# A graph network on one core: the tensor engine no longer stops for its own every seventh select to mark a choice buffer as used

## The chip, the cores and the metric

One core of a Trainium2 chip runs one program. The time is device time in microseconds (us) of one execution. The engines are PE (TensorE matmul; PEld is its weight load), DVE (VectorE), ACT (ScalarE), POOL (GpSimd) and SP (SyncE, which here only issues transfers). They run side by side and are ordered by semaphores alone.

## The reference

A graph of 6250 nodes with 128 features and 200,000 edges goes through two blocks, each on top of a layer norm and a residual add:

```python
edge_index = jnp.stack([src, dst])
h = jnp.maximum(_layernorm(x), 0.0)
# block L0: a learned mask for every edge, and a weighted mean of the neighbours
hid = relu(h[src] @ W1[:d] + h[dst] @ W1[d:] + b1)
mask = sigmoid(hid @ W2 + b2)
agg = segment_sum(mask * h[dst], src) / segment_sum(mask, src)
x = x + relu((0.5 * h + 0.5 * agg) @ Wl + bl)
# block L1: four layers; the greatest neighbour, by feature
h = jnp.maximum(_layernorm(x), 0.0)
for layer in range(4):
    agg = segment_max(h[src], dst)
    h = relu(agg @ W + b + h @ R)
x = x + h
```

## The kernel before

Nodes are sorted by their number of edges into 49 tiles of 128, and the tiles into 7 ranges of 7 (896 nodes). A neighbour's row reaches its node in two ways.

The first is a **select** on PE. For each range (7) and each source tile (49) a one-hot matrix of 128 x 896 fp8 values, the choice, picks at most one row of the source tile for each node of the range. The source rows are split into three bf16 parts, so that a select is six matmuls: three parts by two column groups (512 and 384). One pass over all nodes is 7 x 49 = 343 selects. The second way is a **gather** on POOL: an indirect DMA that fetches one row for each of 128 nodes. One pass has 430 of them, into a ring of rows in SBUF.

Two phases use this pattern. Phase A (in the trace from about 819 us to 2229 us) makes the edge masks of block L0: 343 selects. Phase C (from about 3267 us to the end) is the four layers of block L1: 4 x 343 = 1372 selects and 1720 gathers. Between them lies phase B, which the change does not touch.

In phase C the engines do the following, each in an order that was written out by hand.

- PE runs `select(layer, n)` (L2151 to L2170) for n = 0..342. It waits for the choice block when n is a multiple of seven, and for `taken`, so that it is at most three selects ahead of DVE (three PSUM buffers `wide`). Then come six matmuls on L2164; the last counts `selected`. Between selects PE also has the transposes and products of a range (`turn_own` L2147, `turn_staged` L2185, `multiply` L2196 and L2197, `turn_back` L2208).
- DVE runs `take(layer, n)` (L2249, L2252): it waits for `selected` and takes the maximum of `wide` into `even` or `odd`. Between takes it reduces gathered tiles (L2276, L2281) and counts `reduced`.
- POOL runs `gather_tile` (L2032 to L2040; the gather is L2038). Before a tile it waits for the reduction that frees its place in the ring. After a range it stores the new rows (L2049).
- SP runs `load_choice(n)` (L1972 to L1977): a choice block holds seven selects (`CHUNK = 7`), there are three buffers, and the fourth and later loads wait until a buffer is used. Loads of source tiles and own rows stand behind these waits in SP's order.
- ACT converts source tiles and applies bias and relu.

A choice buffer counts as used in this way: after every seventh select PE waits until its own select has been counted and then counts `choice_used`:

```python
last.then_inc(selected, 1)
if s % CHUNK == CHUNK - 1:
    pe.wait_ge(selected, no + 1)
    pe.sem_inc(choice_used, 1)
```

Phase A has the same lines (L1329 to L1331). There the choice is made by DVE (`compare`, L1395 to L1402) three selects ahead of its take, and it is `compare` that waits for `choice_used` at the first select of a block, from the fourth block on. PE has two PSUM buffers in phase A and also the products of `dot`; DVE's take is L1411.

Of the kernel before, what the change touches and what calls it, by code (L numbers as in the profile page):

```python
# [122 lines left out]
def gnn(nc, x_in, src_in, dst_in, w1_in, b1_in, w2_in, b2_in, wl_in, bl_in,  # L123
# [20 lines left out]
    with ExitStack() as whole:  # L144
# [11 lines left out]
        sb, ps, sem = tensors(whole)  # L156
# [51 lines left out]
        with nc.cleanup_on_exit(), ExitStack() as ctx:  # L208
            sb, ps, _ = tensors(ctx)
            sem = nc.alloc_semaphore  # L210
# [168 lines left out]
        with nc.cleanup_on_exit(), ExitStack() as ctx:  # L379
            sb, ps, _ = tensors(ctx)  # L380
            sem = nc.alloc_semaphore
# [295 lines left out]
        with ExitStack() as ctx:  # L677
            sb, ps, sem = tensors(ctx)
# [104 lines left out]
        with ExitStack() as ctx:  # L783
            sb, ps, sem = tensors(ctx)
# [132 lines left out]
        with ExitStack() as ctx:  # L917
            sb, ps, sem = tensors(ctx)
# [105 lines left out]
        CHUNK = RANGE  # L1024
# [48 lines left out]
        with nc.cleanup_on_exit(), ExitStack() as ctx:  # L1073
            sb, ps, _ = tensors(ctx)
            sem = nc.alloc_semaphore
# [37 lines left out]
            parts_made = sem("a_parts_made")  # L1113
            pick_loaded = [sem(f"a_pick_loaded{e}") for e in range(A_PICKS)]
            choice_made = sem("a_choice_made")
            choice_used = sem("a_choice_used")
            choice_stored = [sem(f"a_choice_stored{e}") for e in range(3)]
            selected = sem("a_selected")
            taken = sem("a_taken")
# [186 lines left out]
            @block.tensor  # L1306
            def _(pe):
                def turn_own(a, h, first, count):
                    pe.wait_ge(own_loaded[a], 16)
                    if a or h:  # L1310
                        pe.wait_ge(bt_made, 2 * a + h)
                    for c in range(count):
                        last = pe.transpose(turned[:, c, :], own_b[:, a * RANGE + first + c, :], ident[:, :])
                    last.then_inc(own_turned, 1)

                def select(n):
                    a, s, q, e = n // TILES, n % TILES, n % 2, n // CHUNK % 3
                    if a == 0 and s % CHUNK == 0:
                        pe.wait_ge(parts_made, 3 * (s // CHUNK + 1))
                    pe.wait_ge(choice_made, n + 1)  # L1320
                    if n >= 2:
                        pe.wait_ge(taken, n - 1)
                    for part in range(3):
                        for lo_c, hi_c in ((0, BANK), (BANK, RCOLS)):
                            last = pe.matmul(wide[q][:, lo_c:hi_c], parts[:, s, part, :],  # L1325
                                             choice[e][:, s % CHUNK, lo_c:hi_c], start=(part == 0),
                                             stop=(part == 2))
                    last.then_inc(selected, 1)
                    if s % CHUNK == CHUNK - 1:  # L1329
                        pe.wait_ge(selected, n + 1)  # L1330
                        pe.sem_inc(choice_used, 1)  # L1331

                def dot_own(a):
                    pe.wait_ge(bt_made, 2 * a + 2)
                    if a:
                        pe.wait_ge(masks_made, a)
                    for lo_c, hi_c in ((0, BANK), (BANK, RCOLS)):
                        pe.matmul(logits[:, lo_c:hi_c], minus_w2[:, :],
                                  minus_bt[:, a * RCOLS + lo_c:a * RCOLS + hi_c], start=True, stop=False)

                def dot(a, first, count):

                    pe.wait_ge(taken, a * TILES + first + count)
                    for lo_c, hi_c in ((0, BANK), (BANK, RCOLS)):
                        for s in range(first, first + count):
                            g, row = s % COLS, s // COLS
                            last = pe.matmul(logits[g * WIDTH:(g + 1) * WIDTH, lo_c:hi_c],  # L1347
                                             w2_col[:, WIDTH - 1 - row:2 * WIDTH - 1 - row],
                                             hidden[(a * TILES + s) % A_HIDDEN][:, lo_c:hi_c], start=False,
                                             stop=(s >= TILES - COLS), tile_position=(0, g * WIDTH))  # L1350
                            if lo_c:
                                last.then_inc(dotted, 1)

                def turn_masks(a, h, first, count):
                    pe.wait_ge(masks_made, a + 1)
                    if a or h:
                        pe.wait_ge(masks_copied, 2 * a + h)
                    for c in range(count):
                        last = pe.transpose(mask_turned[:, c, :], mask_t[:, (first + c) * P:(first + c + 1) * P],
                                            ident[:, :])  # L1360
                    last.then_inc(masks_turned, 1)

                for half in HALVES:
                    turn_own(0, *half)
                pe.wait_ge(w_loaded, (3 + 3) * 16)
                pe.wait_ge(w2_clear, 2)
                for n in range(SELECTS):
                    a, s = n // TILES, n % TILES
                    select(n)
                    if s == 0:  # L1370
                        if a:
                            dot(a - 1, FOURS, TILES - FOURS)
                        dot_own(a)
                    elif s % COLS == 0:
                        dot(a, s - COLS, COLS)
                    if a < RANGES - 1 and s in TURN_AT:
                        turn_own(a + 1, *HALVES[TURN_AT.index(s)])
                    for half, at in zip(HALVES, MASK_AT):
                        if a and s == at[1]:
                            turn_masks(a - 1, *half)  # L1380
                dot(RANGES - 1, FOURS, TILES - FOURS)
                for half in HALVES:
                    turn_masks(RANGES - 1, *half)

            @block.vector
            def _(dve):
# [8 lines left out]
                def compare(n):  # L1395
                    m, s = n // CHUNK, n % CHUNK
                    dve.wait_ge(pick_loaded[n % A_PICKS], (n // A_PICKS + 1) * 16)
                    if s == 0 and m >= 3:
                        dve.wait_ge(choice_used, m - 2)
                        dve.wait_ge(choice_stored[m % 3], m // 3 * 16)  # L1400
                    dve.tensor_scalar(choice[m % 3][:, s, :], pick_row[n % A_PICKS][:, :], one_up[:, :], None,  # L1401
                                      ALU.is_equal, saturate=False).then_inc(choice_made, 1)  # L1402
# [79 lines left out]
                for n in range(3):  # L1482
                    compare(n)
# [4 lines left out]
                for n in range(SELECTS):  # L1488
                    a, s = n // TILES, n % TILES
# [73 lines left out]
        with ExitStack() as ctx:  # L1563
            sb, ps, sem = tensors(ctx)
# [327 lines left out]
        with ExitStack() as ctx:  # L1892
            sb, ps, sem = tensors(ctx)
# [29 lines left out]
            far_used = sem("c_far_used")  # L1923
            far_did = sem("c_far_did")
            choice_loaded = [sem(f"c_choice_loaded{e}") for e in range(3)]
            choice_used = sem("c_choice_used")
            source_loaded = [sem(f"c_source_loaded{e}") for e in range(2)]
            rest_made = sem("c_rest_made")
            parts_made = sem("c_parts_made")
            selected = sem("c_selected")  # L1930
# [34 lines left out]
            def _(sp):  # L1965
# [6 lines left out]
                def load_choice(n):  # L1972
                    a, c, e = n // CHUNKS_OF % RANGES, n % CHUNKS_OF, n % 3
                    if n >= 3:
                        sp.wait_ge(choice_used, n - 2)
                    sp.dma_start(choice[e][:, :, :].bitcast(U8),
                                 chosen[a, :, c * CHUNK:(c + 1) * CHUNK, :]).then_inc(choice_loaded[e], 16)  # L1977

# [160 lines left out]
            def _(pe):  # L2139
# [11 lines left out]
                def select(layer, n):  # L2151
                    a, s = n // TILES, n % TILES
                    no, m = layer * SELECTS + n, (layer * SELECTS + n) // CHUNK
                    q, e = no % 3, m % 3
                    if a == 0 and s % CHUNK == 0:
                        pe.wait_ge(parts_made, 3 * (layer * CHUNKS_OF + s // CHUNK + 1))
                    if s % CHUNK == 0:
                        pe.wait_ge(choice_loaded[e], (m // 3 + 1) * 16)

                    if no >= 3:  # L2160
                        pe.wait_ge(taken, no - 2)
                    for part in range(3):
                        for lo_c, hi_c in ((0, BANK), (BANK, RCOLS)):
                            last = pe.matmul(wide[q][:, lo_c:hi_c], parts[:, s, part, :],  # L2164
                                             choice[e][:, s % CHUNK, lo_c:hi_c], start=(part == 0),
                                             stop=(part == 2))
                    last.then_inc(selected, 1)
                    if s % CHUNK == CHUNK - 1:
                        pe.wait_ge(selected, no + 1)
                        pe.sem_inc(choice_used, 1)  # L2170

                def turn_staged(layer, a, h, first, count):
                    no = range_no(layer, a)
# [226 lines left out]
```

## Time and profile before

| | us |
|---|---|
| median of 3 runs | 6895.0 |
| lowest, highest | 6875.02, 6910.07 |
| span of the profiled execution | 6939.9 |

The profiled execution's own time is known by its span, from its first to its last instruction; it lies 44.9 us above the median of the runs.

Busy time by engine in the profiled execution: PE 3939.7 us (57%), DVE 4021.9 us (58%), POOL 3259.7 us (47%), ACT 858.7 us (12%). No engine is busy throughout, so the busy shares alone name no bound; the waits between the engines have to be read. In the timelines consecutive instructions of a kind are merged into one row; matmuls overlap each other, and their ends are modelled. In brackets stands the idle time of the engine before the row and who ended it; "remote" is a release that the profile can't put down to an instruction, "issue" is no wait that it shows.

### The profile page before, as it was taken

How to read it: one execution, taken by the hardware profiler on the slowest of the kernel's cores; microseconds unless marked ns; L12 is line 12 of the kernel's file. 1: busy time of each engine (PE TensorE's matmuls, PEld its weight loads, DVE VectorE, ACT ScalarE, POOL GpSimd, SP SyncE). 2: the span in 40 equal slices, each digit the busy share in tenths (PEclk: the TensorE clock that was granted, in tenths of full speed). 3: DMA queues.
4: the chain of work that ended last, by engine and by line, in shares of the span. 5: the costliest groups of instructions: out<-in, count | busy, mean ns of one | idle time of the engine just before them, and what ended most of it. 6: DMA issues, size and time to landing. Idle time of an engine off the chain costs nothing.

```text
span 6939.9 us, 51665 instructions
## 1 busy us (share of the span) xinstructions
PE 3939.7 (57%) x16577; PEld 1823.3 (26%) x16577; DVE 4021.9 (58%) x6785; ACT 858.7 (12%) x2421; POOL 3259.7 (47%) x3300
## 2 busy tenths in 40 slices
PE   7631255535544698995565554565655565555565
PEld 5411122112211244442222221222222222222232
DVE  7799266535654688885555454454555454454454
ACT  0000000000000567763000001000010000000000
POOL 0300456756766334334455445555446555444544
PEclk9999577767777899997787777777777777687787
DMA  6468444323432899996322223222233222322221
GB/s 252 170 251 327 126 117 120 108 75 106 120 96 77 168 182 200 194 185 137 89 87 87 78 78 90 77 85 78 80 85 86 80 84 78 86 82 79 80 87 59
DMA packets 367939, 820.12 MB, mean 118 GB/s; under 512 B 101885, under 2 KB 222547, under 8 KB 367491
## 3 DMA queue, kind: packets, MB, share of 16 engines
q0 software_dynamic: 145712, 329.41, 21.7%
q1 hardware_dynamic: 172564, 408.70, 17.1%
q10 hardware_dynamic: 49392, 78.70, 3.9%
q8 instruction: 133, 2.18, 0.1%
q14 instruction: 138, 1.13, 0.0%
HBM read 579.98 MB, written 236.57 MB: 118 GB/s over the span
## 4 chain that ended last, share of the span: by engine, by line
PE 20%; another core or an unknown queue 20%; issue 7%; DVE 5%; POOL 0%; DMA 0%; ACT 0%; DVEq 0%; POOLq 0%
PE c_wide L2164 18%; DVE c_even L2252 2%; DVE c_ring L2276 1%; DVE c_odd L2252 1%; PE c_product L2196 1%; PE c_product L2197 1%; DVE c_source L2239 0%; PE c_turned L2208 0%; PE c_turned L2185 0%; DVE c_best_t L2259 0%; POOL table L2049 0%; DVE c_even L2249 0%; DVE c_staged L2281 0%; DMA c_source<-table 0%
## 5 line engine op out<-in xcount | busy, mean ns | idle before, releaser
L2164 PE MATMUL c_wide<-c_choice,c_parts 128*128 128x512 fp8e4 (+1 forms) x8232 | 1909.8, 392 | 1617.2 <-remote 727.9
L2038 POOL DMA_INDIRECT c_ring<-table,near x1720 | 1657.7, 964 | 995.4 <-issue 521.4
L2164 PEld LDWEIGHTS c_wide<-c_choice,c_parts 128*128 128x128 bf16 x8232 | 835.3, 106 | 2666.0 <-issue 1565.2
L2252 DVE TENSOR_TENSOR c_even<-c_even,c_wide 128x896 f32<-128x896 f32 x672 | 728.3, 1084 | 834.9 <-remote 635.6
L2252 DVE TENSOR_TENSOR c_odd<-c_odd,c_wide 128x896 f32<-128x896 f32 x644 | 698.0, 1084 | 778.1 <-remote 568.3
L1325 PE MATMUL a_wide<-a_choice,a_parts 128*128 128x512 fp8e4 (+1 forms) x2058 | 512.9, 398 | 506.2 <-DVE a_hidden L1411 265.5
L1411 DVE TENSOR_TENSOR a_hidden<-a_wide,a_minus_bt 128x896 f32<-128x896 f32 x343 | 372.0, 1085 | 623.3 <-remote 492.0
L1204 POOL DMA_INDIRECT a_ring<-table_a,near x430 | 470.1, 1093 | 450.1 <-DVE a_value L1472 279.3
L1733 PE MATMUL b_agg<-b_mass,b_h_row 128*128 128x512 f32 (+1 forms) x1372 | 595.3, 571 | 140.7 <-DMA b_mass<-masks 140.1
L1694 ACT ACTIVATE b_mass<-b_onehot,mask_r 128x128 f32<-128x128 bf16 x2058 | 625.5, 387 | 265.0 <-DVE b_onehot L1756 264.9
L1672 POOL DMA_DIRECT2D b_mass<-masks x343 | 297.4, 867 | 548.0 <-ACT b_mass L1694 508.4
L1211 POOL DMA_INDIRECT masks<-a_value,a_cell x430 | 447.2, 1040 | 138.7 <-issue 130.4
L1325 PEld LDWEIGHTS a_wide<-a_choice,a_parts 128*128 128x128 bf16 x2058 | 201.8, 106 | 827.0 <-issue 686.3
L2103 ACT ACTIVATE c_h_t<-c_product,c_b 128x512 f32<-128x512 f32 (+1 forms) x56 | 35.5, 634 | 2848.4 <-PE c_product L2197 2518.2
L1733 PEld LDWEIGHTS b_agg<-b_mass,b_h_row 128*128 128x128 f32 x1372 | 260.1, 198 | 455.5 <-issue 251.4
L2049 POOL DMA_INDIRECT table<-c_new,row_info x147 | 144.2, 981 | 501.2 <-ACT c_new L2112 466.1
L1778 DVE TENSOR_TENSOR b_pile<-b_pile,b_mass 128x896 f32<-128x896 f32 x224 | 244.3, 1091 | 159.4 <-DMA b_mass<-masks 158.7
L1756 DVE TENSOR_TENSOR b_onehot<-pick_of,up_row 128x768 bf16<-128x768 bf16 x343 | 326.2, 951 | 0.1
L1347 PE MATMUL a_logits<-a_hidden,a_w_col 128*32 128x512 f32 (+1 forms) x1372 | 189.4, 649 | 114.6 <-DVE a_hidden L1411 64.3
L2276 DVE TENSOR_TENSOR c_ring<-c_ring 128x256 f32<-128x256 f32 (+8 forms) x468 | 248.4, 531 | 0.3
L1401 DVE TENSOR_SCALAR a_choice<-a_pick_row,one_up 128x896 fp8e4<-128x896 bf16 x343 | 237.4, 693 | 0.0
L707 POOL DMA_INDIRECT meta<-record,rank x49 | 47.2, 963 | 381.8 <-DVE rank L777 367.4
(284 smaller groups left out, 3294.5 us busy)
## 6 DMA issues: line engine op xcount, KB each, us to landing
masks<-n_zeros SPq DMA_DIRECT2D x196, 784.0 KB, 20.5
b_mass<-masks POOLq DMA_DIRECT2D x343, 448.0 KB
c_choice<-chosen SPq DMA_DIRECT2D x196, 784.0 KB
a_pick_row<-picks ACTq DMA_DIRECT2D x343, 224.0 KB
chosen<-a_choice SPq DMA_DIRECT2D x49, 784.0 KB
c_ring<-table,near POOLq DMA_INDIRECT x1720
c_source<-table SPq DMA_DIRECT2D x28, 448.0 KB
a_ring<-table_a,near POOLq DMA_INDIRECT x430
```

The costliest lines, as they stand in the source:

```text
L1204: pool.indirect_dma_start(ring[:, at + j, :], None, table_a, bass.IndirectOffsetOnAxis(near[:, u, j:j + 1], 0)).then_inc(landed[u % A_FLOW ...
L1211: pool.indirect_dma_start(mask_cells, bass.IndirectOffsetOnAxis(cell[:, j:j + 1], 0), value[:, j:j + 1], None).then_inc(cells_stored, 16)
L1325: last = pe.matmul(wide[q][:, lo_c:hi_c], parts[:, s, part, :], choice[e][:, s % CHUNK, lo_c:hi_c], start=(part == 0), stop=(part == 2))
L1411: dve.tensor_tensor(hidden[n % A_HIDDEN][:, :], wide[n % 2][:, 0:RCOLS], minus_bt[:, a * RCOLS:(a + 1) * RCOLS], ALU.max).then_inc(taken, 1)
L1672: pool.dma_start(flat[e], masks[u * P:(u + 1) * P, cb * RCOLS:(cb + 1) * RCOLS], accum_op=ALU.add).then_inc(mass_loaded[e], 16)
L1694: last = act.mul(mass[k % M_RING][:, c, :], onehot[e][:, c, :], mask_r[:, u, cb * RANGE + c:cb * RANGE + c + 1])
L1733: last = pe.matmul(agg[cb % 2][:, lo_c:hi_c], h_row[:, u, :], flat[e][:, lo_c:hi_c], start=(u == 0), stop=(u == TILES - 1))
L1756: dve.tensor_tensor(onehot[e][:, :, :], bc(pick_of[:, u, first:first + SCALED].unsqueeze(2), full), bc(up_row[:, :].unsqueeze(1), full), A ...
L2038: pool.indirect_dma_start(ring[:, at + j, :], None, table1[layer % 2], bass.IndirectOffsetOnAxis(near[:, u, j:j + 1], 0)).then_inc(landed[ ...
L2164: last = pe.matmul(wide[q][:, lo_c:hi_c], parts[:, s, part, :], choice[e][:, s % CHUNK, lo_c:hi_c], start=(part == 0), stop=(part == 2))
L2252: dve.tensor_tensor(side[:, :], side[:, :], found, ALU.max).then_inc(taken, 1)
L2276: halves.did(dve.tensor_tensor(lower, lower, upper, ALU.max))
```

## The change

PE's wait for its own seventh select and its count of `choice_used` go away in both phases, and so does the semaphore. Who refills a buffer, DVE's `compare` in phase A and SP's `load_choice` in phase C, waits for the count of selects itself: for seven times the number of blocks that must be done.

```diff
@@ phase A, PE select
                     last.then_inc(selected, 1)
-                    if s % CHUNK == CHUNK - 1:
-                        pe.wait_ge(selected, n + 1)
-                        pe.sem_inc(choice_used, 1)
@@ phase A, DVE compare
                     if s == 0 and m >= 3:
-                        dve.wait_ge(choice_used, m - 2)
+                        dve.wait_ge(selected, CHUNK * (m - 2))
                         dve.wait_ge(choice_stored[m % 3], m // 3 * 16)
@@ phase C, SP load_choice
                     if n >= 3:
-                        sp.wait_ge(choice_used, n - 2)
+                        sp.wait_ge(selected, CHUNK * (n - 2))
@@ phase C, PE select
                     last.then_inc(selected, 1)
-                    if s % CHUNK == CHUNK - 1:
-                        pe.wait_ge(selected, no + 1)
-                        pe.sem_inc(choice_used, 1)
```

There are 49 such places in phase A and 196 in phase C.

## Rows read from the trace of the kernel before

**Rows 1.** The page, parts 1 and 2: busy time, and granted clock by slice.
```profile
PE 3939.7 (57%) x16577; PEld 1823.3 (26%) x16577; DVE 4021.9 (58%) x6785; ACT 858.7 (12%) x2421; POOL 3259.7 (47%) x3300
PEclk9999577767777899997787777777777777687787
```

**Rows 2.** Busy time by engine in the first and last layer (granted clock, DMA share, GB/s).
```profile
3270.70:4168.00 897.30, 508.36 (x2249) 234.32 (x2247) 456.52 (x559) 37.69 (x58) 445.89 (x463) 0.76 0.29 83
...
5990.00:6940.00 950.00, 511.17 (x2212) 231.15 (x2212) 467.89 (x576) 27.99 (x35) 468.54 (x486) 0.75 0.28 80
```

**Rows 3.** Line views of L2164 and L2038, and PE's seventh wait, L2170 (ns minimum/median/maximum).
```profile
L2164 PE MATMUL c_wide<-c_choice,c_parts x8232: 323/379/634, 3266.9 to 6906.9; 128*128 128x512 fp8e4 x196
...
L2038 POOL DMA_INDIRECT c_ring<-table,near x1720: 941/947/1824, 3248.6 to 6888.2; - x192
...
L2170 PEldq EVENT_SEMAPHORE  x196: 51/51/51, 3303.1 to 6907.2; - x196
```

**Rows 4.** L2164: idle before it, by releaser (us, times); then who waited for it.
```profile
  remote: 727.9, 53
  DVE c_even L2252: 485.9, 179
...
  PE c_wide L2164: 35.8, 89
...
  PE c_turned L2208: 2.1, 7
  PE c_product L2196: 1.4, 4
```

**Rows 5.** Timeline of PE (start us, us, what), outside POOL's gathers.
```profile
3983.38 3.57 PE L2164 MATMUL c_wide<-c_choice,c_parts 128*128 128x512 fp8e4 x18 [0.30 <-PE c_wide L2164]
...
3988.51 4.70 PE L2164 MATMUL c_wide<-c_choice,c_parts 128*128 128x512 fp8e4 x24
3993.52 0.52 PE L2208 MATMUL c_turned<-ident,c_h_t 128*128 128x128 f32 x3 [0.30 <-PE c_wide L2164]
```

**Rows 6.** Timeline of DVE in the same stretch.
```profile
3984.12 0.95 DVE L2276 TENSOR_TENSOR c_ring<-c_ring 128x768 f32<-128x768 f32 x1
3984.99 1.08 DVE L2252 TENSOR_TENSOR c_even<-c_even,c_wide 128x896 f32<-128x896 f32 x1
...
3993.25 1.09 DVE L2252 TENSOR_TENSOR c_even<-c_even,c_wide 128x896 f32<-128x896 f32 x1
3995.21 1.09 DVE L2252 TENSOR_TENSOR c_odd<-c_odd,c_wide 128x896 f32<-128x896 f32 x1 [0.87 <-PE c_wide L2164]
```

**Rows 7.** DVE's takes (L2252 alone) in and behind one run of gathers, by window.
```profile
3866.00:3875.00 9.00, 6.91 (x7) 1.00 0.43 133
3875.00:3916.00 41.00, 3.96 (x4) 0.59 0.25 69
3916.00:3927.60 11.60, 6.35 (x6) 0.70 0.25 75
```

**Rows 8.** Timeline of PE in that run of gathers.
```profile
3874.06 2.43 PE L2164 MATMUL c_wide<-c_choice,c_parts 128*128 128x512 fp8e4 x12
3886.95 4.64 PE L2164 MATMUL c_wide<-c_choice,c_parts 128*128 128x512 fp8e4 x12 [10.46 <-remote]
...
3917.27 6.40 PE L2164 MATMUL c_wide<-c_choice,c_parts 128*128 128x512 fp8e4 x18 [12.98 <-DVE c_odd L2252]
```

**Rows 9.** Waits of SP's queue and of POOL: us in total, times, longest us.
```profile
SPq L1976 <- PEq L2170: 2839.6, 155, 50.9
...
POOL c_ring L2038 <- DVE c_staged L2281: 469.4, 37, 31.2
POOL table L2049 <- ACT c_new L2112: 466.1, 32, 30.2
```

**Rows 10.** L1325, phase A's select: idle before it, by releaser (us, times).
```profile
  remote: 134.0, 8
...
  PE a_wide L1325: 4.6, 11
```

More of the change, by code:

```diff
@@ L1115, in gnn @@
             choice_made = sem("a_choice_made")
-            choice_used = sem("a_choice_used")
             choice_stored = [sem(f"a_choice_stored{e}") for e in range(3)]
@@ L1925, in gnn @@
             choice_loaded = [sem(f"c_choice_loaded{e}") for e in range(3)]
-            choice_used = sem("c_choice_used")
             source_loaded = [sem(f"c_source_loaded{e}") for e in range(2)]
```

## The prediction, made before the changed kernel was run

> **What bounds the kernel now.** I read the busy shares first: PE and DVE are at 57% and 58%, so neither is full, and PE's granted clock is at seven tenths in most slices of phase C [rows 1]. A layer takes about 910 us with PE busy for 510, DVE for 460 and POOL for 450 to 470 of them [rows 2]. Three engines at half load that wait for each other make a chain, so I went on to the waits of the selects.
>
> PE's idle time before a select has two large parts: DVE's takes (485.9 us for the even ones), and 727.9 us in only 53 stops that the profile gives to nobody [rows 4]. The timeline shows what these 53 are. POOL issues gathers in runs; in the one that begins at 3866 us DVE gets through seven takes in the first 9.0 us, four in the next 41.0 us, while the gathers are in flight, and six (with two copies of a new range beside them) in the 11.6 us behind the run [rows 7]. Nothing else in DVE's order holds it there: each of the four takes starts as soon as its select is counted. PE issued two selects at 3874.06 and the next only 10.46 us after their modelled end [rows 8]. So a select that costs 1.13 us alone takes 7 to 15 us while many gathers are in flight, and PE falls idle enough that the granted clock drops to 0.59 in that window [rows 7]. Over the 78 runs of gathers in phase C it looks the same: about 10 to 14 takes to a run, whether it has 20 gathers or 50.
>
> The chain of phase C is then: in a run of gathers the time is POOL's (1720 gathers at 0.947 us and 0.30 us between them, 2145 us [rows 3]), and PE and DVE nearly stand. Between runs the time is PE's and DVE's: POOL waits for a reduction or for new rows, 469.4 and 466.1 us [rows 9], and the runs can't start before DVE has worked off its order. A microsecond of PE is worth a microsecond between the runs and in their first 9 us, if DVE isn't the later one, and almost nothing inside.
>
> **What the change removes.** At a seventh select PE stops until its own count is back. Rows 5 give the price. Twenty-four matmuls take 4.70 us and eighteen 3.57, so a select is 4.70 - 3.57 = 1.13 us, and the modelled end of a batch lies 3.57 - 3 x 1.13 = 0.18 us behind the place where the next select would begin. With the stop it begins 0.30 us after that end. One stop costs 0.30 + 0.18 = 0.48 us of PE. The wait's own instruction (51 ns [rows 3]) lies within it. If each of the 245 stops in both phases were paid in full, the gain would be 245 x 0.48 = 118 us; that is the upper end, and zero is the lower.
>
> How many are on the path:
> - In phase C 89 + 7 + 4 = 100 stops are ones in which PE's own select was what came last [rows 4], 48 us gross. DVE hides some. After the stop before 3983.38 DVE has a reduction of 0.95 us and takes the next select without a gap: hidden. After the one before 3993.52 DVE waits 0.87 us for PE: paid [rows 5, 6]. To count them all I laid phase C out select by select from the same records: a select starts at the latest of the select before it plus 1.13, the third take back, and (at a seventh) its own completion; a take starts at the later of its select and DVE's order; all that these terms don't explain stays as recorded. Without the own-completion term 75 of the 100 stops shorten the end, by 33.5 us together.
> - In 43 of the other 96 the profile names another releaser or none, but the same gap of 0.30 us mostly stands there. They give 12 us by the same reckoning.
> - The last 53 fall into stalls of gathers [rows 4]. Taken at face value they give 26 us. But inside a run the wall time is POOL's: work that PE begins 0.48 us earlier crawls 0.48 us longer. At the speed of rows 7 (four takes in 41 us, against one in 1.13) a tenth of it is left, some 3 us. Both ends, 3 and 26, go into the range; I take 3, since in rows 7 the takes stand still until the gathers have landed.
> - Phase A has 11 stops of this kind, 4.6 us of idle time [rows 10]. It has two PSUM buffers, so DVE's take is nearly always the later one; the reckoning gives 2 us, and 6 more at stalls, of which I take none.
>
> Sum: 33.5 + 12 + 3 + 2 = 50 us of 6939.9.
>
> **What it adds.** SP waits for `selected` in place of `choice_used`. It is still the seventh select that releases it, now by its own count and not by PE's instruction behind it, so a load is issued up to 0.1 us earlier. Behind that wait stand the loads of own rows and source tiles; none comes later. SP waits for the seventh select 155 times already [rows 9], and the buffer that it fills is needed two blocks, at least 14 x 1.13 = 16 us, later. Nothing is late next there: no row puts a PE stop down to a choice load. In phase A `compare` waits for select 7(m-2) when DVE has already taken select 7m-4: the wait is always met, and an equal wait stood there before. I cost both at nothing. If the cover went away, the price would be that of a late load, the length of a transfer.
>
> What is late next, once PE doesn't stop, is DVE: a take is 1.08 us at 1.0 us spacing when queued, plus reductions, against 1.13 us for a select. The two are so close that DVE is already behind at a quarter of the stops.
>
> **A rule weighed against the row.** The row says 0.48 us for a stop [rows 5]. The Trainium skill, "TensorE: Matmul & The Clock Gate", section "Single matmul latency", gives an isolated matmul (398 + N)/2.4 ns at the high clock, so the part that a stream hides is 398/2.4 = 166 ns; its section "Part 2: What happens when you issue a matmul" says that the drain of one matmul overlaps the fill of the next. If only that came back, 143 stops would be worth 0.166 us each, 24 us gross and 18 net by an estimate from this page, and the time would be about 6877. The 0.18 us of overlap in rows 5 agrees with it; the 0.30 us are on top of it, and the rule doesn't speak of them.
>
> **The rivals.**
> - *The stops inside the stalls count too.* If a stalled select has a fixed length from the moment it is issued, then issuing earlier brings all of it forward. For it: the 53 stops stand in front of long stalls. Against: the stalls end with the runs. Gain 33.5 + 12 + 26 + 8 = 80 us, time 6815.
> - *DVE or another wait takes the stop's place.* The layout keeps every other wait as recorded; if DVE's lag after a stop spreads more than it says, half or less of 50 is left, 10 to 30 us, time 6865 to 6885. For it: at 25 of the 100 stops it is so now, and the select behind a seventh also waits for a choice block and `taken`.
> - *Only the overlap comes back.* The next instruction has counted waits too (`taken`, a choice block); if reading them costs PE the 0.30 us of [rows 5] in any case, only 0.18 us of a stop are saved: 143 x 0.18 = 26 us, of which three quarters are on the path, 19 us, time 6876. Against it: selects within a block wait for `taken` and follow each other without a gap [rows 5]. The rule above gives nearly the same, 6877.
> - *Slower: the runs of gathers grow together.* Each run has 9 us in which PE and DVE go on at full speed, seven takes, before the stall sets in [rows 7]. Seven takes outside cost 7 x 11.6/8 = 10 us. POOL waits 69 times [rows 9]; if DVE frees the ring a little earlier, POOL may not come to rest and two runs become one, which loses one such start. From five lost starts on the 50 us are gone, and from nine on (90 - 50 = 40 us) the kernel is slower by over 0.5%, 6935. Against: the waits are 469.4/37 = 12.7 and 466.1/32 = 14.6 us long on average, and 0.48 us in seven selects closes only the shortest.
> - *It does nothing.* PE's next instruction waits for something that comes at the same moment: 6895.
>
> **How the numbers follow.** The profiled span is 6939.9, the median 6895.0; 50 us off the span are 0.72%, and 0.72% off 6895 give 6845. A measurement of this kernel can tell about 0.5% from no change, 34.5 us, so that "faster" begins at 6860.5. Chances: forecast (6830 to 6860, with a few runs just above) 0.46; stalls count too 0.18; DVE or another wait in its place 0.20; only the overlap comes back 0.05; runs grow together 0.07; nothing 0.04. Faster is the first two without the forecast's upper edge, 0.46 + 0.18 - 0.02 = 0.62; slower 0.07; the rest, 0.31, is the same. The range runs from 6800 (80 us and the 15 us by which the median can be off) to 6890 (10 us of gain, less 5 of scatter); it leaves out the slower case, no change at all and a little below.
>
> **What would show it.** In the profile after: no instruction on L2170's place; PE's "idle ended by its own select" near zero; rows like 3993.52 without the 0.30; DVE's idle time put down to L2164 down by some tens of us; the four layers shorter by about 12 us each, phase A by 2. The time in the 53 stalls should not change. A layer that is shorter by 20 us would say that the stalls count; fewer runs of gathers with longer ones among them would say that they grew together; unchanged layers with DVE idle less and PE idle more on `taken`, that DVE took the stop's place. The forecast is wrong if the stalls aren't tied to the gathers but to PE's own queue, since then the change reaches them.

## The result, and the profile after

The changed kernel takes 6807.1 us (median of 4 runs, 6786.0 to 6819.5), the kernel before beside it 6885.2 us. The ratio is 0.9874 with a 95% interval of 0.983 to 0.9917: 1.3% faster. In a later series it was 6807.6 against 6908.0 us, 0.9889 (0.9848 to 0.993). The forecast had the sign, and the time lies in its range, but the gain is 78 to 100 us where 50 were forecast.

First the page of the profile after, parts 1 and 2. Its span is 6809.3 us, 1.7 us below that execution's own time.

```profile
span 6809.3 us, 51420 instructions
...
PE 3987.8 (59%) x16577; PEld 1827.2 (27%) x16577; DVE 4012.4 (59%) x6785; ACT 858.9 (13%) x2421; POOL 3264.0 (48%) x3300
...
PEclk9999578776777798998777777777767776777777
```

The instruction counts are those of [rows 1], and the busy times lie within 50 us of them; it is idle time that is gone. The two spans differ by 131 us, more than the medians do, because the profiled execution of before was a long one.

The view of PE's select line in phase C: who ended its idle time (us, times).

```profile
L2159 PE MATMUL c_wide<-c_choice,c_parts x8232: 323/379/634, 3249.9 to 6776.6; 128*128 128x512 fp8e4 x196
...
  issue: 1819.0, 1702
  DVE c_odd L2244: 872.4, 250
  DVE c_even L2244: 665.6, 244
```

The rows of [rows 4] in which PE waited for itself (89 + 7 + 4 times) are gone, and so are the 53 that the profile gave to nobody. The idle time of these 53, 727.9 us, is not gone with them: most of it now stands under DVE's takes (1538.0 us against 873.2 before), so the stalls of PE in the runs of gathers are still there. What moved is their place. By the records PE sat idle for 1617 us before selects in the kernel before, 897 of it ahead of the first select of a block; after, it is 1466 us, and 284 of it there. The timeline of PE over a seventh select shows the change best.

```profile
3950.67 4.70 PE L2159 MATMUL c_wide<-c_choice,c_parts 128*128 128x512 fp8e4 x24
3955.21 0.49 PE L2200 MATMUL c_turned<-ident,c_h_t 128*128 128x128 f32 x3
3955.54 4.70 PE L2159 MATMUL c_wide<-c_choice,c_parts 128*128 128x512 fp8e4 x24
```

In [rows 5] the same three transposes stand 0.30 us behind the modelled end of the select before; here they begin 4.54 us after a batch that lasts 4.70, 0.16 us ahead of its end. From one batch's start to the transposes it was 5.01 us and is now 4.54, so the stop was worth 0.47 us, as predicted.

The waits of POOL and of SP's queue (us in total, times, longest us):

```profile
POOL table L2044 <- ACT c_new L2107: 443.3, 24, 31.3
POOL c_ring L2033 <- DVE c_staged L2273: 382.2, 35, 29.4
...
SPq L1971 <- PE c_wide L2159: 2039.0, 136, 46.1
```

POOL rests 110 us less between its gathers than in [rows 9] (443.3 + 382.2 against 466.1 + 469.4). SP waits for the select directly, as the last line shows.

Last the view that corresponds to [rows 7]: DVE's takes in and behind a run of gathers of the same length at the same place of the first layer, first the 9 us from its start, then 41 us, then 9 us.

```profile
3826.70:3835.70 9.00, 7.54 (x7) 1.00 0.43 135
3835.70:3876.70 41.00, 5.47 (x6) 0.64 0.25 69
3876.70:3885.70 9.00, 4.33 (x4) 0.76 0.46 140
```

In the 41 us there are six takes and not four. The run of [rows 7] begins with seven indirect stores of new rows (L2049, from 3865.98 us); its first gather is issued at 3874.99 us. So where this document speaks of a run of gathers, the stores that lead into it belong to it, and the 9 us count from the first of them.

The following table is reckoned from the instruction records of each trace: the time from a layer's first to its last take, added over the four layers, and the takes that fall between 9 us after a run of gathers has begun and 3 us after it has ended. A run is a row of indirect transfers of POOL, stores too, with no gap over 0.6 us. The pace outside is the rest of phase C's time, with the three changes of layer of 32 us each in it, divided by the rest of the takes; without these changes all its figures are about 0.08 us lower and their differences stay.

| trace | stops in C | four layers, us | takes in runs | us a take outside |
|---|---|---|---|---|
| before | 196, with count | 3542 | 336 | 1.601 |
| after | none | 3427 | 390 | 1.551 |
| e1_c_only | none | 3408 | 401 | 1.549 |
| e2_a_only | 196, with count | 3514 | 351 | 1.583 |
| e3_one_back | none, held one select back | 3410 | 403 | 1.547 |
| e4_stop_twice | 392, no count | 3494 | 380 | 1.618 |
| e5_stop_only | 196, no count | 3480 | 379 | 1.570 |
| e6_count_only | count, no stop | 3447 | 380 | 1.531 |
| e7_stop_third | 196, no count | 3429 | 405 | 1.574 |
| e8_stop_every | 1372, no count | 3589 | 338 | 1.758 |
| f1_after_again | none | 3408 | 398 | 1.533 |
| f2_stop_count | 196, with count | 3517 | 354 | 1.576 |
| f3_two_wide | none, two buffers | 3545 | 382 | 1.689 |

Traces of one program differ by some 20 us in the four layers (3408 to 3427 for the changed kernel, which was profiled twice). Phase A scatters more: 1345 to 1438 us over these traces, whether it has stops or not. The takes in runs hang on the definition in two rows: with gaps up to 1.0 us still counted as one run, e8_stop_every has 404 and f3_two_wide 390, while the others move by one at most.

### The profile page after: what moved, and what is told of

Its sections match the earlier page's. It is cut to its first block, busy times and chain, and to the rows that moved or that the text cites. A ratio compares the mean times of both kernels' runs of the same rounds, so it can differ in the third digit from the quotient of the medians.

```text
span 6809.3 us, 51420 instructions
## 1 busy us (share of the span) xinstructions
PE 3987.8 (59%) x16577; PEld 1827.2 (27%) x16577; DVE 4012.4 (59%) x6785; ACT 858.9 (13%) x2421; POOL 3264.0 (48%) x3300
## 3 DMA queue, kind: packets, MB, share of 16 engines
q0 software_dynamic: 145712, 329.41, 22.1%
q14 instruction: 138, 1.13, 0.0%
## 4 chain that ended last, share of the span: by engine, by line
PE 21%; another core or an unknown queue 19%; issue 7%; DVE 5%; DMA 0%; POOL 0%; ACT 0%; SPq 0%; DVEq 0%; POOLq 0%; ACTq 0%
PE c_wide L2159 19%; DVE c_even L2244 2%; DVE c_odd L2244 1%; DVE c_ring L2268 1%; PE c_product L2188 1%; PE c_product L2189 1%; DVE c_source L2231 0%; PE c_turned L2200 0%; PE c_turned L2177 0%; DMA c_source<-table 0%; POOL table L2044 0%; DVE c_best_t L2251 0%; DVE c_staged L2273 0%; ACT c_parts L2084 0%
## 5 line engine op out<-in xcount | busy, mean ns | idle before, releaser
L2159 PE MATMUL c_wide<-c_choice,c_parts 128*128 128x512 fp8e4 (+1 forms) x8232 | 1949.9, 397 | 1467.2 <-issue 636.8
L2044 POOL DMA_INDIRECT table<-c_new,row_info x147 | 147.1, 1000 | 480.8 <-ACT c_new L2107 443.3
```

## The experiments

Each series ran on one chip beside the kernel before. The record numbers the chips 2 (e1 to e4), 3 (e5 to e8), 3 again (e9 to e12), 8 (f1 to f4) and 10 (f5, f6). Where a diff says phase C, phase A is that of the changed kernel.

### Where the gain comes from

**e1_c_only and e2_a_only.** The changed text of phase C with the old phase A, and the reverse.

> The change in phase C alone; phase A keeps its 49 stops. Theory S (a stop costs PE 0.48 us wherever it stands, and inside a run of gathers it also costs progress of the stalled select, seen in the trace of after as 390 takes within runs against 336): nearly all of the 78 us come from phase C, so 6815 to 6825 us. Rival P (the prediction's own working: stops inside the runs are free, 48 us from phase C): 6837 us, and the rest of the 78 us would have to come from phase A.

> The change in phase A alone; phase C keeps its 196 stops. Theory S: phase A is 18 us shorter in the pair of traces, so 6865 to 6880 us. Rival P: 2 us, so 6883 us, the same as before.

Phase C alone: 6798.1 us against 6902.1, ratio 0.9844 (0.9801 to 0.9887). Phase A alone: 6900.9 us, ratio 0.9987 (0.9958 to 1.0016). All of the gain is in phase C. The 18 us that the first pair of traces showed in phase A were scatter; the forecast's 2 us can't be told from nothing. P's figure for phase C, 48 us, is too low by half against 104 us here. Theory S missed both times too: it took the 78 us for phase C and counted on 18 us from phase A.

### What a stop costs

**e3_one_back.** PE is held at a seventh select, but for the select before it.

```diff
                     last.then_inc(selected, 1)
+                    if s % CHUNK == CHUNK - 1:
+                        pe.wait_ge(selected, no)
```

> The changed kernel, and in phase C PE waits at every seventh select for the select before the one it has just issued, so that it is held but never runs empty. Theory S in the form 'an empty PE is what costs': one select is always in flight, so the time is that of the changed kernel, 6807 us, and the takes within runs stay near 390. Rival D (what counts in a run is how many selects PE has issued ahead): the hold takes one of two or three issued selects away, so part of the loss comes back, 6825 to 6850 us, with the interval before the take behind a seventh select above 5.4 us.

6803.0 us, the same as without any hold, with 403 takes in runs. The hold costs nothing as long as one select is in flight. So it is not the waiting instruction that costs; e7 below shows that not every stop that lets PE run empty costs something either.

**e5_stop_only, e6_count_only, e9_stop_count, f2_stop_count.** The two halves of the removed lines apart, and both together with SP left on its new wait.

```diff
 e5_stop_only
+                    if s % CHUNK == CHUNK - 1:
+                        pe.wait_ge(selected, no + 1)
 e6_count_only
+                    if s % CHUNK == CHUNK - 1:
+                        pe.sem_inc(choice_used, 1)
 e9_stop_count, f2_stop_count
+                    if s % CHUNK == CHUNK - 1:
+                        pe.wait_ge(selected, no + 1)
+                        pe.sem_inc(choice_used, 1)
```

> The changed kernel with one stop in seven in phase C (behind the seventh select) but without the count: SP still waits for the selects. Phase C alone was worth about 100 us, and 392 stops cost 87 us. Theory F (the first stop in seven costs all, the second is hidden or pays little): the loss is back, 6890 to 6905 us. Rival C (the stop costs 87/392 = 0.22 us each, and the rest of the 100 us was the count and who waits for it): 6807 + 196 x 0.22 = 6850 us.

> The changed kernel in which PE counts an extra semaphore at every seventh select of phase C, without waiting and with nobody waiting for the count. Theory F: one more short instruction on PE's sequencer, nothing, 6800 to 6815 us. Rival C: if the count is what cost, some of the 100 us come back, 6840 us or more.

> The changed kernel with PE's stop and count back in phase C and SP waiting for the selects. Where the kernel before takes about 6895 us: 6890 to 6905 us if PE's restart of 0.47 us is all there is, 6825 to 6845 us if SP's wait for the count made part of the loss. Where it takes about 5559 us: the same as before.

The stop alone: 6834.3 us against 6896.5, ratio 0.9905 (0.9873 to 0.9937), so about 27 us of the loss are back if e6 and e7, at 6805.2 and 6804.1 us, stand for the changed kernel in this series. The intervals of the ratios of e5 and e6 (0.9833 to 0.9894) overlap, so these 27 us are hardly clear of the scatter; e5 lies below what either theory expected. The count alone: 6805.2 us, nothing. Both: 6906.7 us against 6908.0, ratio 0.9997 (0.9968 to 1.0026), and everything is back. So PE's side is the whole of it, and SP's wait has no measurable part. By the records a stop alone lets PE's next matmul start 0.387 us after the start of its last one, against 0.163 without a stop: 0.22 us lost. With the count behind the wait it is 0.629 us: 0.47 us lost. Without a wait the count leaves it at 0.163 us (e6); why it costs 0.24 us more behind one was not tested. In phase C 196 stops of 0.22 us are 43 us gross, and 27 were paid; 196 of 0.47 us are 92 us gross, and 99 were paid (f2 against f1).

**e4_stop_twice, e7_stop_third, e8_stop_every.** Stops without a count behind the third and the seventh select, behind the third alone, and behind all.

```diff
 e4_stop_twice
+                    if s % CHUNK in (2, CHUNK - 1):
+                        pe.wait_ge(selected, no + 1)
 e7_stop_third
+                    if s % CHUNK == 2:
+                        pe.wait_ge(selected, no + 1)
 e8_stop_every
+                    pe.wait_ge(selected, no + 1)
```

> The changed kernel, with two stops in seven selects in phase C (behind the third and the seventh), twice as many as the kernel before had there. Theory S: about 68 us for 196 stops, so 392 stops give 6807 + 2 x 68 = 6943 us. Rival P: 48 us for 196 stops, so 6807 + 96 = 6903 us. If stops cost less when there are more of them (DVE's lag hides the second), below 6900 us.

> The changed kernel with one stop in seven behind the third select in place of the seventh, in phase C. If a stop costs the same wherever it stands, this equals the one behind the seventh. Theory F in the form 'a stop behind the seventh costs more, since the select behind it also waits for a choice block': 6820 to 6850 us here against 6890 to 6905 there. Theory S (0.48 us plus the lost progress in runs): the same in both places, 6870 to 6900 us.

> The changed kernel with a stop behind every select of phase C, 1372 of them. At 0.48 us of PE each, a select costs PE 1.13 + 0.48 = 1.61 us, above DVE's 1.08 us plus reductions, so nearly every stop between the runs is paid: about 1000 takes x 0.48 = 480 us less DVE's part, 7100 to 7300 us. If PE's look-ahead is what carries a select through a run of gathers, more: above 7300 us. If the cost saturates as from 196 to 392 stops, below 7000 us.

6894.2, 6804.1 and 6982.7 us. All three lie below what was expected of them by the price of 0.48 us. The timeline of PE in e8_stop_every shows four selects with a stop each in 5.41 us where they take 4.70 without, 0.71 / 3 = 0.24 us a stop (0.386 - 0.163 = 0.22 us by the records of all of them):

```profile
4025.15 5.41 PE L2159 MATMUL c_wide<-c_choice,c_parts 128*128 128x512 fp8e4 x24
```

I had counted 0.48 us for these stops too; without the count they are half as dear. 1372 stops of 0.22 us are 302 us gross, and 176 are paid. One stop in seven behind the third cost nothing that can be seen, behind the seventh about 27 us, and both about 90 (e4 against e1 and e3): by the medians more than the two apart. Theory F fails in its first form, since a second stop in seven costs more than the first. What fits is that a small bubble goes into the slack between PE and DVE and a larger one doesn't, but that was only argued; nor is it settled that the third place differs from the seventh, as the intervals of e5 (0.9873 to 0.9937) and e7 (0.9856 to 0.9922) overlap.

### Whether the gathers are what slows the selects

**e9_stop_count, e10_nogather_stop, e11_nogather_free, e12_two_wide.** In this series the kernel before itself took 5558.9 us; everything in it has to be read against that number. In e10 (the kernel before) and e11 (the changed kernel) POOL issues no gathers in phase C. DVE sets the ring to zero once and reduces what lies there, so the gathered neighbours are missing from the output:

```diff
                     if after > 0:
                         pool.wait_ge(reduced, after)
-                    for j in range(CAP[u]):
-                        pool.indirect_dma_start(ring[:, at + j, :], None, table1[layer % 2],
-                                                bass.IndirectOffsetOnAxis(near[:, u, j:j + 1], 0)
-                                                ).then_inc(landed[n % FLOWS], 16)
...
-                        dve.wait_ge(landed[n % FLOWS], LANDED[n])
```

> The changed kernel with PE's stop and its count back at every seventh select of phase C, while SP still waits for the selects: PE as before, SP as after. In the traces a stop alone makes PE restart 0.387 us after the start of its last matmul, against 0.163 without one (0.22 us lost), and a stop with the count behind it 0.629 us (0.47 us lost). Theory P2 (PE's restart is all there is): the whole loss is back, 6890 to 6905 us. Rival W (SP's wait for the count made part of the loss): as the stop alone, 6825 to 6845 us.

> The kernel before without the 1720 gathers of phase C: the ring is set to zero once, the reductions run on it, and the output lacks the neighbours that come by gathers. If gathers slow the selects, phase C falls from 3540 us to PE's and DVE's own time; DVE has 1855 us of work in 3669, so about 2100 to 2300 us for phase C and 5400 to 5700 us in all. If the long stalls have another cause (code, loads of choices), phase C stays above 3000 us.

> The changed kernel without the gathers of phase C, beside the kernel before without them. Phase A is worth nothing by its own run, so the difference is that of 196 stops with no run of gathers near. Price-only theory: 0.47 us each if all are paid, 91 us, three quarters paid 68 us. Theory R (about half of the loss comes from stops inside runs of gathers): with the gathers gone only what is paid between runs is left, but now for all stops; 40 to 70 us less than the kernel before without gathers. If DVE is the later engine throughout, under 20 us.

> The changed kernel with two PSUM buffers for selects in phase C in place of three, so that PE is at most two selects ahead of DVE. If what PE has issued ahead carries selects through a run of gathers, fewer takes fall into runs (below 370 against 390) and the time is above 6850 us. If look-ahead doesn't matter inside the runs, PE loses only between them, where a reduction of 0.3 to 0.95 us holds it back: 6810 to 6850 us.

In this series the gathers ran without slowing PE as they do in the others. The page of e9_stop_count, its gathers (with who waited for them), and PE's stops:

```profile
PE 3741.0 (67%) x16577; PEld 1776.8 (32%) x16577; DVE 4003.7 (72%) x6785; ACT 859.8 (15%) x2421; POOL 3320.5 (60%) x3300
...
PEclk9999958878787759989997999989898989889887
```

```profile
L2034 POOL DMA_INDIRECT c_ring<-table,near x1720: 940/944/2112, 3029.4 to 5537.4; - x192
...
  issue: 529.6, 1714
...
  DVE c_ring L2272: 490.8, 133
```

```profile
  PE c_wide L2160: 45.1, 147
```

POOL gathers almost without rest (its wait for a reduction is 0.6 us, against 469.4 in [rows 9]), a layer takes 574 to 588 us, and it is DVE that waits for gathers, 490.8 us, which it never did before. e9_stop_count equals the kernel before to 1.0001 (0.9992 to 1.001). Both have the same 196 stops, 147 of them with PE waiting for itself, so this says again that SP's wait has no part; it does not say what the stops cost here. With two buffers and no stops (e12) the ratio is 1.0034 (1.0021 to 1.0047). The changed kernel itself wasn't run in this series, and what the change is worth in it was not measured.

Nothing ties this to a chip. The record gives this series and the one before it, twelve minutes earlier, the same chip number 3, and the kernel before took 6896.5 us there (11 runs) and 5558.9 us here (16 runs). Phase A shows it as well: 1138 to 1145 us in this series, and 1338 to 1438 us in all the others.

The expected values of e9 and e12 were written for a kernel before of about 6895 us and can't be judged here. e10 came out below its own: phase C took 1947 us from first to last take where 2100 to 2300 were expected. Without gathers the pair e10 and e11 gives 5028.8 and 5000.0 us: 196 stops of 0.47 us are 92 us gross, and 29 are paid. That falls between the two ranges of e11's text; that DVE, the later engine at many stops, hides the rest was argued and not tested.

**f1_after_again, f3_two_wide, f4_nogather_free.** In the next series (chip 8) the kernel before takes 6908.0 us. f1, f2, f3 and f4 are the same programs as the changed kernel, e9, e12 and e11. The diff of f3 leaves out that buffers are now counted modulo 2.

```diff
 f3_two_wide
-            wide = [ps(f"c_wide{q}", [P, 2 * BANK]) for q in range(3)]
+            wide = [ps(f"c_wide{q}", [P, 2 * BANK]) for q in range(2)]
...
-                    if no >= 3:
-                        pe.wait_ge(taken, no - 2)
+                    if no >= 2:
+                        pe.wait_ge(taken, no - 1)
```

> The changed kernel itself, on the chip of this series. In the last series the kernel before took 5559 us and not 6890: the gathers ran there without slowing the selects, POOL gathered without rest, and PE's stops came to nothing. If this series is like the last one, the change is worth nothing: ratio 0.998 to 1.001. If it is like the ones before it (kernel before at about 6895 us), 6800 to 6815 us.

> Two PSUM buffers for selects in phase C in place of three. Where the kernel before takes about 6895 us: above 6850 us and fewer than 370 takes within runs if it is PE's look-ahead that carries selects through a run of gathers, 6805 to 6850 us if not. Where it takes about 5559 us it cost 0.34% in the last series.

> The changed kernel without the gathers of phase C. Where the kernel before takes about 6895 us: if the gathers are what slows the selects there, a layer takes 455 us as it did in the last series, about 5200 us in all; if the slow selects have a cause of their own that was absent in the last series, layers stay above 600 us.

f1 repeats the result (0.9889). f4 took 5263.6 us in its single run, with layers of 457 to 464 us: without gathers phase C runs as it did in the series before (455 us, e11), so it takes the gathers to make the long selects. They are not enough by themselves, as e9 shows. The 264 us by which f4 is slower than e11, the same program, are phase A's, which still has its gathers: 1429 us against 1141. f3 took 6932.0 us, 124 more than the changed kernel (114 without its two longest runs), but with 382 takes in runs against 398; the pace outside is 1.689 us against 1.533. The third buffer is worth a lot, and nearly all of it outside the runs. The time is what rival D expected, the takes in runs are not (it wanted fewer than 370).

**f5_one_part and f6_plain**, one run each, beside 6865.8 us for the kernel before, in one run as well.

```diff
 f5_one_part
-                    for part in range(3):
+                    for part in range(1):
...
-                                             stop=(part == 2))
+                                             stop=True)
 f6_plain
-                        pool.indirect_dma_start(ring[:, at + j, :], None, table1[layer % 2],
-                                                bass.IndirectOffsetOnAxis(near[:, u, j:j + 1], 0)
-                                                ).then_inc(landed[n % FLOWS], 16)
+                        pool.dma_start(ring[:, at + j, :], table1[layer % 2][u * P:(u + 1) * P, :]
+                                       ).then_inc(landed[n % FLOWS], 16)
```

> The changed kernel with one of the three parts in each select of phase C, so that a select is two matmuls and not six, and the result is the bf16 rounding of the rows. Where gathers slow the selects (kernel before at about 6895 us), a take inside a run comes every 5 us or so. If a run of gathers stretches all of PE's work in proportion, that falls to about 2 us and DVE is the later engine nearly everywhere, 5700 to 6000 us in all; a restart of 0.47 us is then stretched too, to about 2 us. If it is a fixed wait for each select or for each restart, takes inside runs stay at 4 to 5 us, and the time stays above 6500 us.

> The changed kernel with each gather of phase C as a plain copy of 128 consecutive rows from the same queue of POOL, same bytes and same places in the ring, so the rows are not the neighbours. Where gathers slow the selects: if it is the traffic into the ring, the layers stay at 840 to 860 us and the runs look the same; if it is the indirect form, the long stops vanish and a layer takes 460 to 600 us.

f5: 6313.0 us, between the two expectations. A take inside a run comes every 2.53 us on average, against 5.06 in f1 (the windows' time over the takes in them); two matmuls for six, half the time.

The long intervals say more. From one take's start to the next within a layer, none in f1 is over 16.8 us, which is reached three times with six matmuls to a select. In f5, with two, 131 of the 273 intervals over 3 us are 5.6 us, a third of that; one is 16.8 us. So at its slowest a run of gathers costs about 2.8 us for each matmul, in proportion to PE's work, and that speaks against a fixed wait for each select or for each count. The intervals also go in steps of 0.70 us (3.55, 4.25, 4.95 and so on to 16.1 and 16.8): in f1 88% of those over 3 us lie between 0.02 us below and 0.10 us above a multiple of 0.70, in f5 94%, in e9 13%, where 17% would by chance. No run shows what keeps this step. The low clock is only a small part of it: twelve matmuls take 2.43 us at the high level and 4.64 us in the run [rows 8], 1.1 us more for a select.

f6: 5186.1 us. The line view of POOL's copies, and busy time by engine over 400 us of the second layer (PE, PEld, DVE, ACT, POOL, granted clock, DMA share, GB/s):

```profile
L2033 POOL DMA_DIRECT2D c_ring<-table x1720: 537/537/713, 3205.0 to 5142.4; - x192
...
DMA to landing us min/median/max: 2.0/2.7/6.6
```

```profile
4000.00:4400.00 400.00, 358.72 (x1784) 173.19 (x1783) 367.68 (x455) 32.71 (x45) 218.34 (x372) 0.97 0.49 148
```

The same bytes from the same queue into the same places leave PE alone. Its clock is at 0.97 and a layer takes 455 to 459 us, as with no gathers; the queue moved as many packets as in f1 (145,712, 329.41 MB). So it is not the amount of traffic that slows PE. The edit changes two things at once, though: the form of the transfer and the rows that it reads, which now follow one another. An indirect gather of consecutive rows, which would tell them apart, was not run.

## Why the prediction held outside the runs of gathers and failed inside them

**The price of a stop** held: 0.48 us predicted from [rows 5], 0.629 - 0.163 = 0.47 us by the records of all stops. What I had not seen is that half of it is the count behind the wait.

**Outside the runs** the reckoning agrees with what was measured. It gave 33.5 + 12 = 46 us. The pace outside the runs is 1.601, 1.583 and 1.576 us in the three traces with stops and counts, and 1.551, 1.549, 1.533 and 1.547 in the four without: 0.042 us less over about 1000 takes, 42 us. Traces of one kind differ by up to 0.025 us, so by an estimate from that scatter this is 42 us give or take some 15.

**Inside the runs** is the term that was mis-sized: 3 us, out of a range of 3 to 26. The three traces with stops have 347 takes in runs on average, the four without 398. These 51 takes needn't be done outside at 1.545 us each, 79 us; the windows themselves are some 10 us shorter with stops, so about 70 us come from here. 42 + 70 are the 111 us by which the layers differ (3524 against 3413 us on average). The step that failed is "inside a run the wall time is POOL's: work that PE begins 0.48 us earlier crawls 0.48 us longer". The first half holds: the runs of gathers add up to 2440 to 2454 us in all seven traces. But the stop doesn't stay 0.48 us there. Inside runs, and with the first takes of the layers left out, the take behind a seventh select comes 5.70, 5.36 and 5.66 us after the one before it (before, e2, f2) and 3.50, 4.09, 3.38 and 4.02 us without a stop (after, e1, f1, e3). So a stop costs 1.8 us there: it is stretched like the work. And since the runs are as long as before, what isn't taken in them has to be taken outside at full price.

That is half of it. Some 52 stops of 1.8 us are 95 us of time in runs, 19 takes at 5.1 us. The other half shows in the six other takes of a block: inside runs they come 4.95, 4.82 and 4.75 us apart with stops and 4.57, 4.34, 4.50 and 4.42 us without, 0.38 us less for some 290 of them, 110 us. So the selects that have no stop of their own are slower too when there are stops. Why is open; how far ahead PE and DVE are when a run begins may be part of it, which no run told apart.

The rival "the stops inside the stalls count too" had 6815 us and was the nearest, but it too took the stops at face value, 26 us for those in the stalls against the 70 measured. It is also what set the lower end of the range, 6800 us. That the measured 6807 us lie inside is therefore partly luck. The prediction had named the sign: 12 us a layer if it was right, 20 us if the stalls count. The layers are shorter by 28 us each on average.

**Phase A** was right to be near nothing, and **the added waits** were free: SP's wait has no part in the loss (f2). **The rival that runs of gathers grow together** didn't come about: with the definition above there are 79, 76 and 74 runs in the three traces with stops and counts, 75 or 76 in the four without. **DVE or another wait in the stop's place** is true in part: without gathers 29 of 92 us are paid (e10, e11). With gathers 78 to 104 us come back, as much as the gross 92 us, which isn't the sum of paid stops but 42 outside and 70 inside.

**The rule weighed against the row.** The Trainium skill, "TensorE: Matmul & The Clock Gate", section "Single matmul latency", gives 398/2.4 = 166 ns for the part that a stream hides. The 0.16 us by which matmuls overlap here agree with it; taken as the whole price of a stop it would have given 6877 us, and the measurement decides against that.

**The last sentence of the prediction** named what would make it wrong: that the stalls aren't tied to the gathers. They are tied to them (f4, f6), so the step failed with that premise standing.

## What to carry to other kernels

Before pricing a bubble (a short idle time) on an engine, find out whether the engine's work is stretched somewhere: here the bubble was stretched there too, and it isn't free just because another engine sets the wall time, since every unit of work that isn't done there has to be done later. PE paid twice for waiting for its own last instruction, once for running empty and once for the count that stood behind the wait, so let the consumer wait on the count that exists already. And read the kernel before beside every result: the same program took 5559 us in one series and about 6900 us in the others, one of these on a chip of the same number, and what the change is worth at 5559 us nobody measured.

## What the runs showed of the hardware

- Indirect gathers from POOL (128 rows of 512 bytes each, one every 1.25 us) slow PE's selects from about 9 us after a run of indirect transfers begins until about 3 us after it ends: a select of 1.13 us then takes 4.3 to 5.1 us on average and up to 16.8 us (19.0 once). The slowing deepens with the run: in the 46 runs of over 25 us in the trace of before there are 0.8 takes a us at first and fewer than 0.1 in the last 8 us. At its slowest it is about 2.8 us for a matmul, and it goes in steps of 0.70 us (f1, f5).
- The granted clock is 0.59 in the 41 us of [rows 7], a mean over its two levels; PE was busy for 10.4 us of them.
- Plain copies of the same size from the same queue don't slow PE (f6), and in one series the gathers didn't either (5559 us), though the chip number is that of the series before. What in the gathers does it, and what that series was free of, stays open.
- A plain copy from POOL occupies it for 0.537 us, an indirect one for 0.947 us and 0.30 us of idle time behind it.
- A wait of PE for its own last matmul costs 0.22 us from start to start (0.386 against 0.163 us), and a count behind the wait another 0.24 us (0.629); a count without the wait cost nothing that can be measured (0.163 us, e6).
